# A graph network on one core: the edge terms of layers 1 to 4 are finished in the second pass and stored in place of their activations

## The reference

```python
for l in range(5):
    h = leaky(x @ W1[l] + b1[l]) @ W2[l] + b2[l]
    e = leaky(edge_attr @ We1[l] + be1[l]) @ We2[l] + be2[l]
    msg = h[src] * e * dot_scale[l]
    agg = segment_sum(msg, dst)
    x = layernorm(x + agg * res_w[l]) * ln_g[l] + ln_b[l]
```

## Time and profile before

| what | value |
|---|---|
| median of 3 runs | 6621.7 us (6618.35 to 6628.33) |
| profiled execution | 6654.04 us, span 6652.2 us |
| mean granted TensorE clock | 0.882 |
| busy: PE, PEld, DVE | 79%, 73%, 79% of the span |
| busy: ACT, POOL | 63%, 76% of the span |

### The profile page before, as it was taken

The page is one execution under the profiler, slowest core; times in us unless marked ns, Lnnn a source line. Parts: engine busy times, 40 slices in busy tenths (PEclk is TensorE's granted clock), DMA queues, the critical chain, the costliest instruction groups (busy, mean ns, idle before and its releaser), DMA issues. The chain is left out here.

```text
span 6652.2 us, 143082 instructions
## 1 busy us (share of the span) xinstructions
PE 5234.0 (79%) x53270; PEld 4875.2 (73%) x53270; DVE 5252.9 (79%) x12225; ACT 4172.9 (63%) x6886; POOL 5051.2 (76%) x6785
## 2 busy tenths in 40 slices
PE   7999863333433799997999988999979999799996
PEld 6888752222222688997989887898978898788896
DVE  8887786666766688887888877888878888788886
ACT  4777636665666366665666665666646666466664
POOL 6777777777777477776777776777767777677776
PEclk9999976655555799998999998999979999799998
DMA  4444337877877333332333332333323333233332
GB/s 108 115 112 111 99 88 242 262 260 240 281 264 263 95 101 97 100 101 77 95 99 99 101 93 76 100 100 100 98 70 100 100 101 98 69 100 100 100 101 69
DMA packets 503715, 828.89 MB, mean 125 GB/s; under 512 B 110094, under 2 KB 217221, under 8 KB 489966
## 3 DMA queue, kind: packets, MB, share of 16 engines
q1 hardware_dynamic: 373374, 656.68, 29.4%
q0 software_dynamic: 129648, 163.06, 13.5%
HBM read 384.92 MB, written 434.48 MB: 123 GB/s over the span
## 5 line engine op out<-in xcount | busy, mean ns | idle before, releaser
L720 POOL DMA_INDIRECT gring<-tableh,src_i x2525 | 2476.3, 981 | 895.7 <-issue 597.9
L1391 PE MATMUL psum<-penalty,arena 125*128 125x192 bf16 x25755 | 2425.2, 247 | 268.9 <-DVE es_w L1792 78.3
L1391 PEld LDWEIGHTS psum<-penalty,arena 125*128 125x128 bf16 x25755 | 2160.0, 98 | 342.5 <-ACTq L1036 208.4
L1792 DVE TENSOR_SCALAR arena<-dst_f,node_id 125x768 bf16<-125x768 f16 x4301 | 1767.6, 458 | 0.1
L720 POOL DMA_INDIRECT gring<-table,src_i x1313 | 1336.7, 1018 | 448.8 <-issue 348.0
L706 POOL MEMSET diag<- 128x256 f32 x2712 | 1016.4, 375 | 107.9 <-ACT es_w L916 3.6
L1003 ACT COPY psum<-diag 128x512 f32<-128x512 f32 x505 | 297.6, 590 | 1244.1 <-DVE psum L1838 731.3
L1832 DVE TENSOR_REDUCE gring<-psum 128x192 f32<-128x576 f32 x505 | 378.1, 749 | 337.8 <-remote 208.0
L1855 DVE TENSOR_TENSOR_SCAN by_lane<-mask_x,psum 128x256 f32<-128x256 f32 x1010 | 630.9, 663 | 0.2
L1013 ACT COPY run<-by_lane 128x512 f32<-128x512 f32 x505 | 565.9, 1121 | 97.2 <-ACT gring L1032 42.1
L1167 PE MATMUL psum<-ident,by_lane 128*128 128x128 f32 x202 | 66.6, 433 | 699.9 <-DMA by_lane<-attr_last 465.0
(11 more groups left out here) (283 smaller groups left out, 8806.4 us busy)
## 6 DMA issues: line engine op xcount, KB each, us to landing
rows<-arena SPq DMA_DIRECT2D x101, 1296.0 KB
acts<-arena SPq DMA_DIRECT2D x505, 256.0 KB
arena<-acts SPq DMA_DIRECT2D x505, 256.0 KB
rowsg<-run SPq DMA_DIRECT2D x505, 256.0 KB
dst_f<-pe_src SPq DMA_DIRECT2D x608, 93.8 KB
gring<-tableh,src_i POOLq DMA_INDIRECT x2525
rows<-run SPq DMA_DIRECT2D x101, 256.0 KB
gring<-table,src_i POOLq DMA_INDIRECT x1313
```

Of the source, the lines that this page charges most:

```text
L720: pool.indirect_dma_start(ring[:, s, k, :], None, table, bass.IndirectOffsetOnAxis(ap=src_i[:, c * K + k:c * K + k + 1], axis=0))\
L1391: ins = mm(found(n)[:, m, :], hot_at(n // 2, j)[:, at:at + P], parts[:, j, :, :].rearrange("q a f -> q (a f)"), start=(j == 0), stop=(j == ...
L1792: ins = ts(hot_at(pair, j), src_row[b], node_id[:, j:j + 1], None, ALU.is_equal)
```

## The change

The second half of the edge term of layers 1 to 4 is computed in the second pass. After its first halves of chunk c+1, PE makes four groups of four products for chunk c (`second_products`), from the activations still in SBUF. Products of even number go to PSUM bank 6 and are finished by DVE, which adds the bias while it writes them back over the activations (`finish_e`, in steps 0 and 2 of `gat_chunk`). Those of odd number go to bank 7, which ACT presets with the bias (`preset_e`) and then copies back (`evict_e`). SP stores the finished terms where it stored the activations. The ring for them has three places for two (`RING`). The weights `We2` and biases `be2` are loaded ahead of the second pass, after a memset by POOL.

In layers 1 to 4 PE has look-ups alone, ACT presets nothing, and DVE multiplies the loaded term in SBUF with the gathered rows. The load of a place of the ring waits for DVE's multiplication four chunks before. Layer 0 is as it was. Buffers move: `We2` stands in `dst_f`, the first source row in a new tile `early`, some constants share a tile `once` with two one-hot rows. Functions for widths (`kp`, `pair_width`, `gathered`, `T_PARTS`) are more general and give the numbers of before.

```diff
@@ SP
-            store_acts(CH)
+            sp.wait_ge(zero_set, 1)
+            sp.wait_ge(bc4_used, 2)
+            for q in range(2):
+                half = slice(q * F, (q + 1) * F)
+                sp.dma_start(e2_all[half, :, half], We2.rearrange("l d e -> d l e")).then_inc(pack_in, 16)
+            sp.dma_start(be_all, be2.partition_broadcast(P)).then_inc(pack_in, 16)
             for c in range(CH):
                 if c + 3 < CH:
                     load_nat(CH + c + 3)
-                if c + 1 < CH:
-                    store_acts(CH + c + 1)
+                store_acts(CH + c)
                 sp.wait_ge(gat_steps, (c + 3) * K)
                 sp.dma_start(chunk_rows(rows2, c, WG), run2[:, c % 2, :, :]).then_inc(rows2_out[c % 2], 16)
@@ SP, store_acts
-                    sp.wait_ge(ya_sb, nth(g, i) + 1)
+                    if a == 0:
+                        sp.wait_ge(ya_sb, nth(g, i) + 1)
+                    else:
+                        sp.wait_ge((e_sb_dve, e_sb_act)[i % 2], 2 * c + i // 2 + 1)
@@ SP, load_edges
-                if n >= SL:
-                    sp.wait_ge(e_ready, n - SL + 1)
+                if SL <= n < SL + CH:
+                    sp.wait_ge(e_ready, ET * CH + n - SL + 1)
+                elif n >= SL + CH:
+                    sp.wait_ge(edge_steps, msg_done(n - SL))
@@ ACT
+            def preset_e(c, h):
+
+                if c or h:
+                    act.wait_ge(e_sb_act, 2 * c + h)
+                copy(e_bank(1).rearrange("p (k f) -> p k f", f=F),
+                     be_all[:, LH + 2 * h + 1:LH + 2 * h + 2, :].to_broadcast([P, K, F])).then_inc(be_set, 1)
+
+            def evict_e(c, h):
+
+                act.wait_ge(e_ready, ET * c + 2 * h + 2)
+                settle()
+                copy(pass_of(CH + c)[4][:, 2 * h + 1, :], e_bank(1)).then_inc(e_sb_act, 1)
@@ ACT, messages
+                    if k == 1 and c:
+                        evict_e(c - 1, 0)
+                        preset_e(c - 1, 1)
                 copy(msg2[:, s % 2, :, 0:F], gather2[:, s, :, 0:F]).then_inc(hopcopy, 1)
                 if c + 2 < CH:
                     copy_attr(CH + c + 2)
+                if c:
+                    evict_e(c - 1, 1)
+                    preset_e(c, 0)
                 if c + 1 < CH:
                     leaked(CH + c + 1)
@@ PE
+            def second_products(c):
+
+                ring = pass_of(CH + c)[4]
+                for i in range(ET):
+                    pe.wait_ge(ya_sb, nth(CH + c, i) + 1)
+                    if i % 2:
+                        pe.wait_ge(be_set, 2 * c + i // 2 + 1)
+                    elif c or i:
+                        pe.wait_ge(e_sb_dve, 2 * c + i // 2)
+                    settle()
+                    for u in range(4):
+                        at = ((u % 2) * 2 + u // 2) * P
+                        ins = mm(e_bank(i)[:, u * P:(u + 1) * P], ring[:, i, at:at + P], e2_all[:, LH + i, :],
+                                 start=(i % 2 == 0), stop=(i % 2 == 0 or u == 3), skip_group_check=True)
+                    ins.then_inc(e_ready, 1)
...
             for c in range(CH):
                 if c + 1 < CH:
                     transpose_attr(CH + c + 1)
                 first_halves(CH + c)
+                if c:
+                    second_products(c - 1)
+            second_products(CH - 1)
...
                 for c in range(CH):
-                    second_half(c)
+                    if l == 0:
+                        second_half(c)
                     look_up(c)
@@ DVE
+            def finish_e(c, h):
+
+                dve.wait_ge(e_ready, ET * c + 2 * h + 1)
+                l = LH + 2 * h
+                tt(pass_of(CH + c)[4][:, 2 * h, :].rearrange("p (k f) -> p k f", f=F), e_bank(0).rearrange("p (k f) -> p k f", f=F),
+                   be_all[:, l:l + 1, :].to_broadcast([P, K, F]), ALU.add).then_inc(e_sb_dve, 1)
@@ DVE, gat_chunk
                     prev = run2[:, s % 2, k, :]
+                    if k in (0, 2):
+                        finish_e(c, k // 2)
                     if c + 1 < CH and k < L - LH:
                         leaky_edges(CH + c + 1, k)
@@ DVE, edge_chunk
-                    dve.wait_ge(e_ready, n + 1)
+                    if n < CH:
+                        dve.wait_ge(e_ready, ET * CH + n + 1)
+                    else:
+                        dve.wait_ge(act_ready[s], 16 * (n // SL + 1))
+                    terms = psum[:, 2 + b, :] if n < CH else act_in[:, s, :]
```

More of the change, by code:

```diff
@@ L49 @@
 NJA = 17
-HOT = NJA * WIDE[0]
+NJB = 17
+HOT0 = NJA * WIDE[0] // 2
+HOT = HOT0 + NJB * WIDE[1] // 2
+ET = L - 1
+RING = (2, 3)
 AL = 4
@@ L80 @@
 CE = P
-CW = CN + CE
+CW = CN
 CE1 = 2 * P
@@ L240, in build @@
         row_of = sb("row_of", [NQ, NJ])
-        shift = sb("shift", [P, P])
-        bound = sb("bound", [P, P])
+        once = sb("once", [P, (WIDE[0] + WIDE[1]) // 2])
+        shift, bound, below, above = (once[:, i * P:(i + 1) * P] for i in range(4))
+        pen_m = once[:, 4 * P:6 * P].rearrange("p (a n) -> p a n", a=2)
         spare = sb("spare", [P, NJ])
         ident = sb("ident", [P, P])
-        below = sb("below", [P, P])
-        above = sb("above", [P, P])
         ones = sb("ones", [P, P])
@@ L370, in kp, with gathered, pair_width, e_bank @@
         def kp(n):
-            return KPE[n % 4]
+            return 3 if n < CH else KPE[n % 4]
+        def gathered(n):
+            return 16 * sum(K - kp(m) for m in range(n % SL, n + 1, SL))
+        def pair_width(pair):
+            return (kp(2 * pair) + kp(2 * pair + 1)) * P
+        def e_bank(i):
+            return psum[:, 6 + i % 2, :]
         def hot_at(pair, j):
@@ L495, in _ @@
                     sp.wait_ge(src_T_sb, 1)
-                    for i in range(3):
+                    for i in range(T_PARTS):
                         rows = min(P, PE_COLS - i * P)
@@ L762, in _ @@
             gather_nodes(rows1, agg_all, agg_in)
+            pool.wait_ge(hot1_done, (CH + 1) // 2)
+            pool.wait_ge(hot1_act, (CH + 1) // 2 - 2)
+            pool.memset(e2_all, 0.0).then_inc(zero_set, 1)
             pool.wait_ge(t2_out, NG * 16)
@@ L872, in leaked @@
                         act.wait_ge(ya_sb, nth(g, i) - 1)
-                    if c >= 2:
-                        act.wait_ge(act_out[a][c % 2], 16 * layers * (c // 2))
+                    d = c - RING[a]
+                    if d >= 0:
+                        act.wait_ge(act_out[a][d % 2], 16 * layers * (d // 2 + 1))
                         settle()
@@ L1025, in one_hot_act @@
                     at = (n - 1) * 2 * some
-                    slices = [hot_at(pair, NV + half * some + d) for d in range(some)]
+                    wide = pair_width(pair)
+                    slices = [hot_at(pair, NV + half * some + d)[:, 0:wide] for d in range(some)]
                     for d in range(some):
-                        nc.scalar.activation(slices[d], src_row[b], ACT.Abs,
+                        nc.scalar.activation(slices[d], src_row[b][:, 0:wide], ACT.Abs,
                                              bias=minus_id[:, NV + half * some + d:NV + half * some + d + 1]).then_inc(hot_abs, 1)
@@ L1036, in one_hot_act @@
                         act.sem_inc(hot_act, 1)
-                act.wait_ge(e_open, l + 1)
-                preset(0)
-                preset(1)
+                if l == 0:
+                    act.wait_ge(e_open, 2)
+                    preset(0)
+                    preset(1)
                 spread_mask(0)
@@ L1044, in edge_acts @@
                         spread_mask(c + 1)
-                    if c + 2 < CH:
+                    if l == 0 and c + 2 < CH:
                         preset(c + 2)
@@ L1936 @@
 N_WEIGHTS = 3 + 1 + 1 + 4
-N_PACK = 4 + 2 + 1
+N_PACK = 4
+N_EDGE = 3
 N_CONSTS = 21
```

94 lines of the change are left out of this document (52 added, 42 removed).

## The result

| | before | after |
|---|---|---|
| median | 6620.8 us (6618.35 to 6628.33, 4 runs) | 6848.3 us (6844.46 to 6855.55, 4 runs) |
| ratio | 1 | 1.0346, 95% interval 1.0333 to 1.0358 |
| profiled execution | 6654.04 us, span 6652.2 | 6844.46 us, span 6842.7 |
| mean granted TensorE clock | 0.882 | 0.874 |

The change costs 227 us. 181 us were forecast. The time lies inside the range of 6615 to 7000, 45 us over the predicted 6803.

What follows compares the result with a forecast made beforehand. POOL was taken as the bound, with a loop of waits replacing it in the second pass. 155 us (13.2 against 11.65 a chunk) + 7 + 19 = 181, so 6621.7 + 181 = 6803 us; range 6615 to 7000.

Steps and rivals of the forecast that it cites:

- POOL bounds the layers, removals are worth nothing: Layers 1 to 4: POOL's unbroken stream hides the removed 436 us of PE and 238 us of ACT; costed at 0.
- The port, 19 us: Layers 1 to 4: DVE's multiplication with both inputs in SBUF can hold up gathers; 19 us, bounds 0 to 279.
- The full price: Layers 1 to 4: whole 0.69 us of each multiplication holds up gathers, 279 us; rival, in full or part, chance 0.08.
- The port in the second pass: Second pass: no cost was entered; its gathers, 37 ns longer than the layers', only served to scale the layers' term.
- A loop ACT, PE, DVE, ACT replaces POOL's pace: Second pass: waits through product 3 and product 0 set the chunk, 11.6 us at full clock, 15.5 at low.
- The clock: Second pass: PE's bursts begin low about half the time; 12.65 us a chunk, between 11.6 and 13.7.
- Stalls, 0.53 us a chunk: Second pass: ACT's "remote" waits, 1.07 us a chunk, count once slack is gone; half taken, 0.53.
- ACT's slack: Second pass: 2.35 us a chunk of waiting for gathers, eaten entirely by 2.56 us of new presets and evictions.
- the 13.7: Second pass, burst beginning low: product 3 starts at 3.6 us, clock rises after 4.3, product 0 done at 10.2.
- Ends, 7 us: End of the second pass: last chunk's additions, product chain and store of the running sums; 7 us, bounds 1.4 and 12.

Runs made afterwards that it cites:

- e4: Changed kernel with second products, bias fills, evictions and additions left out of the second pass, ring of two: 6635.2 us, ratio 1.0028.
- e6: Kernel of e5 with the loaded term of layers 1 to 4 copied by ACT to PSUM, where DVE reads it: 6657.6 us, ratio 1.0045.
- e8: The kernel before, unchanged, profiled a second time: 6631.3 us, span 6629.5.
- e5: The kernel of e1 run once more, as a base on the same chip: 6669.4 us, ratio 1.0065.
- e1: Changed kernel with DVE's two additions moved behind its leaky steps, from k = 0 and 2 to 3 and 5: 6658.9 us, ratio 1.0066.
- e2: Changed kernel with ACT's eviction of product 1 and second bias fill moved ahead of the weighting of k = 0 and 1: 6679.7 us, ratio 1.0094.
- e3: Changed kernel with 18 bf16 products into an unused PSUM bank where PE waits for the second bias fill: 6691.2 us, ratio 1.0111.
- e12: Kernel of e3 with product 3 of each second-pass chunk computed three times more into an unused bank: 7137.2 us, ratio 1.0725.
- e9: Changed kernel with four extra products per second-pass chunk into an unused bank, ahead of product 3: 6851.1 us, ratio 1.0353.
- e10: Changed kernel with four extra products per second-pass chunk into an unused bank, ahead of product 1: 6853.5 us, ratio 1.0357.
- e7: Kernel of e5 with four columns, not three, looked up by PE in every fourth chunk of layers 1 to 4: 6576.5 us, ratio 0.9918.
- e11: Kernel of e7 with the term copy to PSUM of e6 added: 6550.8 us, ratio 0.9899.

## Why the prediction came out as it did

- **POOL bounds the layers, removals are worth nothing: right.** e4 shows it directly.
- **The port, 19 us: right in size.** e4 has 17 and e6 gives 12 back; by the profiles the layers took 5 us more (e8 against the changed kernel) and 8 less with the copy (e5 against e6). The full price would have been 279. The working was cruder than its result: 1018 ns is the mean of both passes ahead of the layers, and the second profile has 1010 and 984 ns, which by the same working give 13 us.
- The Trainium skill ("SBUF — State Buffer", Who interferes with whom) says that a vector instruction with two SBUF inputs contends with a GpSimd instruction that reads SBUF, over a lock that one of them holds alone; it adds, as an inference, that `tensor_tensor` leaves free the interface that descriptor generation needs. These gathers lie between the two: one in ten of those that overlap the multiplication is held up (40 of 397), none where it reads PSUM.
- **The port in the second pass: put at nothing, and it is not.** I had costed it for the layers alone. The gathers of the two passes ahead of the layers have a mean of 1010 ns in e4 and e8 and of 1024, 1036 and 1046 in e1, e2 and e3. There POOL is the bound again, so it is paid: 14 to 36 ns x 1313 = 18 to 47 us, most of what separates these three from e4 (24 to 56 us). The additions on DVE, which read PSUM and SBUF, are not what holds the gathers up: gathers that overlap them and no operation with two SBUF inputs have the shortest mean, 943 to 946 ns. The long ones (over 1.2 us, of the last 805 of the second pass: 72 in e8, 97, 161 and 189 in e1, e2 and e3) nearly all overlap DVE's weighting and running sum, which the kernel before has too and which now meet the gathers at other moments; those that overlap the weighting have a mean of 1066 ns in e8, 1092 in e1 and 1221 in e2 and e3.
- **A loop ACT, PE, DVE, ACT replaces POOL's pace: right,** by three ways to open or shorten it (e1, e2, e3) and one to lengthen it at a nearly constant clock (e12, 0.93 against 0.96).
- **The clock: here the number failed.** I had worked out 13.7 us for a burst that begins low and 11.6 for a full clock, and took the half, 12.65. The pause is 4.45 us, and all 98 bursts began low. This step is 1.0 us a chunk, 100 us, too small. The rule of the Trainium skill that I named ("TensorE: Matmul & The Clock Gate", HAM oscillation: a pause between bursts throttles again, each burst starts cold) agrees with the trace and would have given 13.7. That the period is 13.65 us is not shown by the sum alone: e9 and e10 have the same period with more work, so the clock's steps hold it too.
- **Stalls, 0.53 us a chunk: too large.** ACT's "remote" waits did not occur at all, neither in the changed kernel nor in the second profile of before. Clock and stalls together: 13.2 us predicted, 13.63 measured. The base of 11.65 is 11.53 in the second profile. From chunk 1 to chunk 100 that is 1349.2 - 1141.7 = 207 us, where 155 were predicted. A step too small by 100 us was half made good by the stalls that never came; that the time fell inside the range, 45 us from the forecast, owes something to luck.
- **ACT's slack: wrong by the choice of the profile.** The prediction let the copies alone eat it, 2.56 of 2.35 us. It is 3.46 us by e8. The pass is not slower because ACT has too much to do, but because of the loop; that part of the prediction stands.
- **Inside the 13.7, two errors cancelled.** From the weighting to product 3 it was 3.20 us, not 3.6, and from the addition to the next weighting 3.17, not 3.5. The stretch of PE between was 7.28 us, not 6.6, since the clock rose after 6.0 us and not 4.3. At the full clock the same sum is 10.82, not 11.6. So the low clock costs 2.8 us a turn and not 2.1.
- **Ends, 7 us: somewhat too large,** inside the bounds of 1.4 and 12. Second pass 209.9 - 207.5 = 2.4, and 1.9 in the node part.
- Sum by profiles: 207.5 + 4.3 + 5.1 - 3.8 = 213 us. The timed difference is 227. 9 us of the 14 between them are where the profiled executions lie: e8's is 5 us above the median of before on its chip, the changed kernel's 4 us below its own.

## What to carry to other kernels

Work moved into another engine's slack costs what the new waits make of it. Before moving it, follow one iteration around all engines: here the same work costs 40 us in one place of VectorE's list and 227 in another. And work that is taken from engines that do not bound a stage is worth something only when the bound can be moved: four look-ups in every fourth chunk turned 43 us of loss (e5) into 49 us of gain (e7), 68 with the term in PSUM (e11). And profile the kernel before twice: one execution had stalls that the next did not, and with them another slack.

## What the runs showed that I had not expected

- A loop that waits with TensorE's clock can keep its period exactly (13.65 us) while 2 us of TensorE work are put on it or beside it (e9, e10). Extra work on such a path is no test of whether it is critical, unless the clock is kept up (e3, e12).
- 18 useless bf16 products in a pause of 4.45 us a chunk took the loss from 227 to 73 us (e3).
- A gather has no fixed price. With no edit of POOL's list its mean ahead of the layers went 1010, 1024, 1036, 1046 ns (e4, e1, e2, e3), with the operations of DVE that it met; in the layers it went from 989 to 1004 ns when PE and DVE got 2% of the span busier (e7).
